# LayerNorm's inverse root: a square root on ScalarE and a reciprocal, or an integer guess and Newton steps on VectorE

## The reference

```python
def _layernorm(x, axis=-1, eps=1e-05):
    m = jnp.mean(x, axis=axis, keepdims=True)
    v = jnp.var(x, axis=axis, keepdims=True)
    return (x - m) / jnp.sqrt(v + eps)

x = x + attn_a(_layernorm(x), W1, b1, Wp, bp)           # causal, 16 heads of 16
x = x + ffn(_layernorm(x), w_gate, w_up, w_down)        # silu(gate) * up, 768 hidden, int weights / 127
x = x + attn_b(_layernorm(x), Wq, Wk, Wv, Wo, k0, v0)   # window of 64 keys, 16 heads of 16
x = x + ffn(_layernorm(x), w_gate, w_up, w_down)
```

## Time and profile before

| what | value |
|---|---|
| median of 3 runs | 1563.59 us (1560.1 to 1564.39) |
| profiled execution, its own time | 1562.93 us |
| its span, first to last instruction | 1561.2 us |
| TensorE busy | 1320.3 us, 85% |
| VectorE busy | 1025.8 us, 66%, 1626 instructions |
| ScalarE busy | 760.4 us, 49%, 1133 instructions |
| GpSimd busy | 404.8 us, 26% |
| mean granted TensorE clock | 0.927 of full speed |

### The profile page before, as it was taken

One profiled execution on the slowest core, in us unless ns is written; L12 is line 12 of the kernel. 1 busy time (PEld: TensorE's weight loads), 2 busy tenths in 40 slices (PEclk: granted clock), 3 DMA queues, 4 the chain that ended last, 5 costly groups with the idle time before them and its releaser, 6 DMA issues.

```text
span 1561.2 us, 24108 instructions
## 1 busy us (share of the span) xinstructions
PE 1320.3 (85%) x9473; PEld 819.6 (53%) x9473; DVE 1025.8 (66%) x1626; ACT 760.4 (49%) x1133; POOL 404.8 (26%) x387
## 2 busy tenths in 40 slices
PE   2698879896899987989698987988788988798968
PEld 2533338654763325855583332775477333386547
DVE  4687655856588746675669773675567876567563
ACT  2426664444434675536352667453545266644534
POOL 1302223201340223411232123330234022232013
PEclk9969999998988999999896999999899799999979
DMA  7620111714170021252325011152235201217120
GB/s 290 202 65 16 57 69 41 188 33 140 50 187 5 24 95 62 56 134 72 135 82 123 9 63 62 49 136 61 85 116 144 62 16 56 71 42 186 56 86 28
DMA packets 86336, 134.87 MB, mean 86 GB/s; under 512 B 24176, under 2 KB 59312, under 8 KB 82992
## 3 DMA queue, kind: packets, MB, share of 16 engines
q1 hardware_dynamic: 86208, 133.09, 28.6%
HBM read 51.45 MB, written 11.61 MB: 40 GB/s over the span
## 4 chain that ended last, share of the span: by engine, by line
PE 54%; DVE 22%; ACT 9%; DMA 5%; issue 5%; POOL 4%; SPq 1%; POOLq 0%; ACTq 0%; DVEq 0%
DVE peak L591 13%; PE opsum L1069 11%; PE ring L1042 7%; PE ring L1019 6%; PE ring L1103 6%; PE ring L1104 6%; PE ring L987 5%; ACT probs L832 4%; PE opsum L1117 2%; PE opsum L1120 2%; PE ring L907 2%; DMA on_lo<-onf 2%; DMA on_lo<-osb 1%; PE ring L921 1%; DVE rest L574 1%
## 5 line engine op out<-in xcount | busy, mean ns | idle before, releaser
L832 ACT ACTIVATE probs<-ring 128x768 f32<-128x768 f32 (+5 forms) x496 | 400.8, 835 | 395.2 <-PE ring L1042 255.6
L591 DVE TENSOR_REDUCE peak<-ring 128x4 f32<-128x768 f32 (+7 forms) x480 | 462.6, 1004 | 156.3 <-PE ring L987 152.9
L1019 PE MATMUL ring<-k_st,q_st 96*128 96x192 bf16 (+4 forms) x1280 | 280.8, 328 | 48.8 <-DVE peak L591 39.6
L1042 PE MATMUL ring<-q_st,k_st 98*128 98x512 bf16 (+5 forms) x1344 | 249.5, 296 | 35.9 <-DMA q_st<-peak_b 13.2
L1069 PE MATMUL opsum<-probs,V 128*32 128x192 f32 (+5 forms) x2816 | 224.4, 413 | 11.5 <-POOL probs L517 8.9
L1042 PEld LDWEIGHTS ring<-q_st,k_st 98*128 98x128 bf16 x1344 | 94.1, 99 | 192.9 <-ACT probs L832 66.3
L1019 PEld LDWEIGHTS ring<-k_st,q_st 96*128 96x128 bf16 x1280 | 101.3, 102 | 172.8 <-DVE peak L591 93.1
L517 POOL TENSOR_SCALAR_AFFINE_SELECT probs<-probs 128x512 f32<-128x512 f32 x128 | 81.4, 636 | 396.6 <-ACT probs L832 396.6
L529 POOL TENSOR_TENSOR h_lo<-hid,h_hi 128x512 fp32r<-128x512 f32 x96 | 123.6, 1291 | 202.1 <-ACT h_hi L866 202.1
L1103 PE MATMUL ring<-xt_hi,w_gu_sb 128*128 128x512 f32 x384 | 154.9, 403 | 21.0 <-issue 12.2
L987 PE MATMUL ring<-mask_a,ident_b 128*128 128x128 bf16 (+2 forms) x704 | 161.5, 283 | 0.0
(11 more groups left out here) (120 smaller groups left out, 1988.4 us busy)
## 6 DMA issues: line engine op xcount, KB each, us to landing
w_gu_sb<-img_gu SPq DMA_DIRECT2D x16, 1536.0 KB, 6.8
w_qkv<-img_qkv SPq DMA_DIRECT2D x8, 1536.0 KB, 8.1
q_st<-q_part SPq DMA_DIRECT2D x96, 128.0 KB, 2.4
q_st<-q_part SPq DMA_DIRECT2D x48, 256.0 KB, 4.7
on_hi<-o_hi SPq DMA_DIRECT2D x64, 128.0 KB, 2.7
k_st<-k_part SPq DMA_DIRECT2D x48, 144.0 KB, 2.5
k_st<-k_part SPq DMA_DIRECT2D x24, 288.0 KB, 7.2
k_st<-k_part SPq DMA_DIRECT2D x48, 128.0 KB, 2.4
```

The lines of the kernel that those rows point to most:

```text
L591: dve.tensor_reduce(peak[:, g % 2, :].rearrange("p (h i) -> p h i", i=NT)[:, h:h + heads, i], heads_of(plan.slot[e], unit, plan.a_width(i) ...
L832: act.activation(probs[:, j % 2, h:h + heads, 0:w], heads_of(plan.slot[e], unit, w), ACT.Exp).then_inc(exp_done, 1)
L1019: pe.matmul(flat(plan.slot[e])[:, per * n + c:per * n + c + d], q, k_st[0:SP_ROWS, HG * g + h0 + n, first_key + c:first_key + c + d], star ...
L1042: last = pe.matmul(flat(plan.slot[e])[:, per * n + c:per * n + c + d], kk, q_st[:, HG * g + h0 + n, q0 + c:q0 + c + d], start=(per * n % 5 ...
```

## The change

`root` and its `std_done` semaphore leave ScalarE, and with them the 15 Sqrt table loads; the Silu load moves up to the place of the Sqrt load at the end of attention. In `scale`, VectorE waits for the aggregated variances and computes the inverse root itself on 128x4 numbers: t = v + eps and half_var = -(v + eps)/2, then the bits of t, as an integer, shifted right by one and subtracted from a constant, which read as a float is a first guess y, and three Newton steps y = y (1.5 - (v + eps) y y / 2) of three operations each. Each operation waits for the one before, but for the second.

```diff
+ROOT_GUESS = float(0x5F3759DF)
...
-                dve.wait_ge(std_done, 2 * base + h + 1)
-                dve.reciprocal(rstd[:, 4 * h:4 * h + 4], std[:, 4 * h:4 * h + 4]).then_inc(rstd_done, 1)
-                dve.wait_ge(rstd_done, 2 * base + h + 1)
+                c = slice(4 * h, 4 * h + 4)
+                y, t, v = rstd[:, c], std[:, c], mv[:, c, 1]
+                at = 13 * (2 * base + h)
+                dve.wait_ge(aggr_done, NT * base + 4 * h + 4)
+                dve.tensor_scalar(t, v, EPS, None, ALU.add).then_inc(rstd_done, 1)
+                dve.tensor_scalar(half_var[:, c], v, EPS, -0.5, ALU.add, ALU.mult).then_inc(rstd_done, 1)
+                dve.wait_ge(rstd_done, at + 2)
+                dve.tensor_scalar(y.bitcast(I32), t.bitcast(I32), 1, None,
+                                  ALU.arith_shift_right).then_inc(rstd_done, 1)
+                dve.wait_ge(rstd_done, at + 3)
+                dve.tensor_scalar(y.bitcast(I32), y.bitcast(I32), -1.0, ROOT_GUESS, ALU.mult,
+                                  ALU.add).then_inc(rstd_done, 1)
+                for n in range(3):
+                    dve.wait_ge(rstd_done, at + 4 + 3 * n)
+                    dve.tensor_tensor(t, y, y, ALU.mult).then_inc(rstd_done, 1)
+                    dve.wait_ge(rstd_done, at + 5 + 3 * n)
+                    dve.tensor_tensor(t, t, half_var[:, c], ALU.mult).then_inc(rstd_done, 1)
+                    dve.wait_ge(rstd_done, at + 6 + 3 * n)
+                    dve.scalar_tensor_tensor(out=y, in0=t, scalar=1.5, in1=y, op0=ALU.add,
+                                             op1=ALU.mult).then_inc(rstd_done, 1)
+                dve.wait_ge(rstd_done, at + 13)
...
-            def root(h, base):
-                act.wait_ge(aggr_done, NT * base + 4 * h + 4)
-                act.activation(std[:, 4 * h:4 * h + 4], mv[:, 4 * h:4 * h + 4, 1], ACT.Sqrt,
-                               bias=EPS).then_inc(std_done, 1)
...
                         if (g, k) == (1, 1):
-                            load_table(ACT.Exp, 4 * a)
+                            load_table(ACT.Exp, 2 * a)
...
-                load_table(ACT.Sqrt, 4 * a + 1)
-                root(0, 2 * a + 1)
+                load_table(ACT.Silu, 2 * a + 1)
                 first_of_turned(0, 2 * a + 1)
-                root(1, 2 * a + 1)
-                load_table(ACT.Silu, 4 * a + 2)
...
                 if a % 2 == 0 or a in next_x:
-                    load_table(ACT.Sqrt, 4 * a + 3)
-                    root(0, n + 1)
                     first_of_turned(0, n + 1)
-                    root(1, n + 1)
                 if a in next_x:
                     first_of_turned(1, n + 1)
...
-            root(0, 0)
-            root(1, 0)
```

More of the change, by code:

```diff
@@ L348, in layers_kernel @@
         rstd = sb("rstd", [P, NT], F32)
+        half_var = sb("half_var", [P, NT], F32)
         sums = sb("sums", [P, 2, 16], F32)
@@ L381, in layers_kernel @@
         names = {}
-        for n in ("x_in qkv_in wp_in gu_in ones_in kpads stats_done aggr_done std_done rstd_done xn_done "
+        for n in ("x_in qkv_in wp_in gu_in ones_in kpads stats_done aggr_done rstd_done xn_done "
                   "turned xhi_done xlo_done qk_ready qk_evac part_hi part_rest part_mid part_lo stack0 stack1 stack2 "
@@ L388, in layers_kernel @@
             names[n] = sem(n)
-        (x_in, qkv_in, wp_in, gu_in, ones_in, kpads, stats_done, aggr_done, std_done, rstd_done, xn_done,
+        (x_in, qkv_in, wp_in, gu_in, ones_in, kpads, stats_done, aggr_done, rstd_done, xn_done,
          turned, xhi_done, xlo_done, qk_ready, qk_evac, part_hi, part_rest, part_mid, part_lo, stack0, stack1, stack2,
```

## The result

After: 1614.38 us, median of 4 runs (1612.98 to 1621.74). Before, on the same chip: 1563.99 us, 4 runs (1560.1 to 1567.72). Ratio 1.0324, 95% interval 1.03 to 1.0348: 3.2% slower, 50 us, where I forecast 2.9% and 46 us. The profiled execution of after took 1614.73 us with a span of 1613.0, against 1562.93 and 1561.2 before. In what follows, a stop is idle time of TensorE in front of an instruction, and a fall is the granted clock going from 1.00 to its lower level.

A forecast was written before the change was run, and what follows sets the result against it. No engine bounds the kernel throughout (TensorE holds 54% of the chain), so each seam was read in place. Delays 4.3 + 7.6 + 2.4 + 1.5 + 15.2 + 10.3 + 4.5 = 45.8 us on 1563.6 gave 1609 us, range 1592 to 1622.

The forecast's parts named there:

- The size of a root: At each call of `scale`: VectorE's chain makes a root 1.9 us longer, 2.15 us where the hop was hidden.
- FFN to windowed attention: Four seams, two calls each: every call delays TensorE's path by 1.9 us, 15.2 us in all.
- (a): Only some seams pay: windowed attention absorbs the second call's 1.9 us and no clock falls; 33.7 us, 1597, chance 0.2.
- Setup: Two calls before the layers, both hops hidden: 2 x 2.15 = 4.3 us.
- Causal attention to FFN: Four seams: first call 7.6 us, second call 2.4 us in layers 2, 4 and 6, slack in layer 0.
- Windowed attention to FFN: Four seams: first call covered by projection 4's DMA wait, second by idle time; only the last layer pays, 1.5 us.
- FFN to next sequence and its clock: Three seams into causal attention: 10.3 us of delay, plus 4.5 us for clock falls after TensorE's 3.6 us stop.
- (b): Clock falls in each new 1.9 us stop at FFN-to-windowed seams, and dear operations: 61 us, 1625, chance 0.15.
- (c): ScalarE's Sqrt table loads were waited for, removal gives back 22.3 us: 1587, chance 0.03; or faster, 1556, chance 0.02.
- (d): Roots hidden behind other VectorE and DMA waits: under 5 us more, chance 0.03.
- The profile: Changed profile: 16 ScalarE loads, no Sqrt, 416 small VectorE instructions, busy near 1085 us, 3.6 us stop at last seam.
- signs of being wrong: Dependent small operations under 0.15 or over 0.23 us start to start, turns starting no later, or clock falls elsewhere.

The follow-up runs named there:

- only_window_ffn: Kernel before with the VectorE root only at the four seams from windowed attention to FFN, table loads kept: 1570.69 us, ratio 1.003.
- only_ffn_next: Kernel before with the VectorE root only in the setup and at the three seams from FFN to next sequence: 1593.37 us, ratio 1.0159.

## Why the prediction was right, and where it was off

**The size of a root** was right in kind and 5% short: 2.0 us instead of 1.9, 2.23 instead of 2.15 where the hop was hidden. The operation's duration, 0.16 us, came out as the slope through two rows gave it; the pause between dependent ones was taken as 0.035 and is that. What I had short is the front: 0.27 us for the first pair where I had 0.21, and 0.41 for the two integer operations where I had 0.37. The Trainium skill's formula for a two-tensor operation (VectorE: DVE Perf Modes, section on the trn2 errata) gives an estimate of 161 ns at 4 elements; the trace agrees, with 162.

**FFN to windowed attention**, the largest term, was right: 15.2 forecast, 15.6 in the trace, 14.4 by the run that changes it alone. Rival (a) had half of it absorbed by the attention behind. Windowed attention gave back 3.4 us in all, not 7.6.

**Setup**: the term was short by 1.3 us for a table load. I counted Sqrt loads in the stream and never asked which instruction would fetch the first table once the root was gone.

**Causal attention to FFN**: 13.3 us in the trace of after where I had 10.0. The two delays are there, but the second was mis-sized. I let the third gate/up unit begin at 993.09, where the turn ends; its first matmul starts at 992.84, before that end, and TensorE starts 0.15 us behind the end of `hid`. With my own 995.8 that gives 995.95 less 992.84, 3.1 us a seam instead of 2.7, and 3.15 is what a seam costs without a fall. Three times 0.45 is 1.4 of the missing 3.3 us; in layers 2, 4 and 6 of after another 1.4 us go with the fall of the clock, and 0.5 us in layer 0 stay unexplained. Changed alone, these seams cost 8.2 us in the medians.

**Windowed attention to FFN**: the step that failed is "TensorE is still at projections 4 and 5 when `xn` is done". It holds only while they run at the lower clock; at full clock the cover is about 1 us, and stops of 0.88 and 1.04 us remain in layers 1 and 3. I had read layer 1 alone and said that the repeats agree within 0.1 us. They do not: the cover in layer 3 of before is 0.96 us against 2.5 in layer 1. Of the 1.5 us that I had put into the last layer, 0.6 came. In all it is 3.9 us where I had 1.5.

**FFN to next sequence and its clock**: 12.7 us where I had 14.8, stops of 3.72 us as forecast (3.6). But the price of the stop does not end at the seam. Filling it shortens the way to the next seam by 10.7 us over three in the traces, of which 1.3 us lie at the seams: my 4.5 us was put at the wrong place and, on this path, too small. What the whole kernel gets back is not clear (4.5 us by the ratio, inside the noise).

**The rivals.** (a) fell: the clock did fall, and the FFN-to-windowed seams changed alone cost 14.4 us. (b) had falls at the FFN-to-windowed seams; at all four the clock stayed at 1.00, behind stops of 1.56 and 1.35 us. Its amount, 61 us, is not reached either. (c) fell with 1.0313 against 1.0312: the loads were early, as ScalarE's idle time in front of the roots said. The Trainium skill (ScalarE: Activation LUTs, section What ACT_TABLE_LOAD costs) prices a change of set with its drain at 2.66 us; even so the 15 that before has more cost nothing that the runs can tell, since they lay in time in which ScalarE waited. (d) fell by a factor of ten.

**The profile** has what I said it would: 16 loads and no Sqrt, 416 small operations, VectorE at 1085 us. Of the signs of being wrong, one came: the clock fell, or stood low for longer, at places that I had not counted.

**Why the total came out near** is partly luck: +1.5, +3.3, +2.4, +0.4 and +4.9 against -2.1, -3.4 and -1.1.

**What stays open**: why the clock stands low for 27 us in the middle of causal attention 2 of after and for 20 in before, at a place where the code is the same. Runs with other edits show both lengths. Nor is it known what decides whether the clock falls behind the stop of a causal seam. The stops of the windowed seam, where projections and DMA alternate, were not filled.

## What to carry to other kernels

Moving a short computation to the engine that produces its input and uses its result saves one hop of 0.5 us, and the chain of 13 operations costs 2.5 us, on 128x4 and on 128x8 alike. Count dependent steps on the path, at about 0.2 us each here, and merge calls that are ready together before looking at the operations. When an early instruction is removed, ask what it had fetched for those behind it. Work out a delay for every repeat of a seam, not for one of them. Read the price of a longer stop of TensorE at the next seam too, and take a local gain of 1 us for a gain only after several runs with their clocks.

## What was not expected of the hardware

- A shorter stop can cost time: 1.48 us down to 0.45 at three places, 3.1 us gained there, and the kernel 0.25% slower, with a mean granted clock of 0.920 instead of 0.928.
- The clock fell 1.5 us into gapless matmul work, behind two stops of 2.12 and 2.28 us that lie 3 us apart (layer 2). One stop alone did either: no fall behind 2.06 us in layer 4 of before and behind 2.28 us in layer 0 of only_window_ffn, a fall behind 1.93 us in layer 2 of only_ffn_next.
- Part of the spread between executions of one kernel is the clock: among 17 of before, 1559.54 to 1571.74 us, the mean clock lies between 0.922 and 0.935, and its correlation with the time is -0.60.
- Transposes that nobody reads kept the clock at 1.00 behind a seam, but delayed the start of the FFN by 0.8 to 1.2 us where they stood ahead of its branch.
